# Moving the re-centring of quantized activations from GpSimd to ScalarE, and reordering one load queue

## The reference

```
B = xn @ W2 + b2;  C = xn @ W3 + b3                  # 16 columns each
delta = softplus(xn @ W1 + b1)                       # 1024 columns
s   = xn * delta * sum_n(B*C)                        # state-space layer, no recurrence left
xh  = xn @ Hadamard(1024) / 32
xq  = clip(round(xh / a), -8, 7) * a                 # a = max|xh| / 7, per token: 4 bits
wq  = ternary(weight) * scale                        # per output row
g   = silu(xq @ wq.T)
out = x + s * g
```

## Time and profile before

| engine | busy us | share of the span |
|---|---|---|
| TensorE (matmul) | 365.7 | 66% |
| VectorE | 384.0 | 69% |
| ScalarE | 307.3 | 55% |
| GpSimd | 327.3 | 59% |

### The profile page before, as it was taken

The page is one execution under the profiler, slowest core; times in us unless marked ns, Lnnn a source line. Parts: engine busy times, 40 slices in busy tenths (PEclk is TensorE's granted clock), DMA queues, the critical chain, the costliest instruction groups (busy, mean ns, idle before and its releaser), DMA issues.

```text
span 554.0 us, 7160 instructions; the slowest of 8 cores (548.4 to 554.0 us)
## 1 busy us (share of the span) xinstructions
PE 365.7 (66%) x1664; PEld 156.1 (28%) x1696; DVE 384.0 (69%) x632; ACT 307.3 (55%) x361; POOL 327.3 (59%) x215
## 2 busy tenths in 40 slices
PE   0005161996987888888888888888888885956400
PEld 0002131442333333333333333333333332422100
DVE  0508888466788887888788788887888866468450
ACT  0622232648676667666666676666666575444320
POOL 5000052151777777777776777776777778687664
PEclk9999565897989888888888888888888898888655
DMA  8993320252444444344444444444444232112101
GB/s 155 240 175 120 114 59 13 65 110 66 120 124 116 118 127 116 114 115 115 114 114 115 115 114 115 118 118 114 119 117 118 61 95 77 58 58 95 57 38 76
DMA packets 80971, 57.98 MB, mean 105 GB/s; under 512 B 70434, under 2 KB 70434, under 8 KB 80930
## 3 DMA queue, kind: packets, MB, share of 16 engines
q1 hardware_dynamic: 72914, 34.39, 27.7%
q0 software_dynamic: 8016, 23.14, 12.6%
HBM read 26.12 MB, written 16.78 MB: 77 GB/s over the span
## 4 chain that ended last, share of the span: by engine, by line
DVE 29%; POOL 26%; PE 18%; DMA 12%; issue 9%; ACT 2%; DVEq 1%; SPq 1%; POOLq 1%; ACTq 0%
POOL ob L33 8%; DVE t1b L33 8%; POOL t4b L33 8%; PE psO L292 7%; DMA xqT<-xqb 6%; PE psO L293 6%; POOL xqb L33 5%; DVE t3b L33 5%; DVE o3s L33 4%; DMA xb<-x 3%; DMA xnT<-xnb 3%; POOL vT L33 3%; DVE tbf L33 3%; POOL uT L33 3%; DVE prod L33 2%
## 5 line engine op out<-in xcount | busy, mean ns | idle before, releaser
L292 PE MATMUL psO<-ternT,xqT 128*128 128x512 bf16 x255 | 121.1, 475 | 68.9 <-DMA xqT<-xqb 66.9
L33 POOL TENSOR_TENSOR t4b<-t3b,o3s 128x1024 f32<-128x1024 f32 x32 | 75.1, 2347 | 85.5 <-DVE t3b L33 85.2
L293 PE MATMUL psO<-ternT,xqT 128*128 128x512 bf16 x256 | 121.4, 474 | 0.8 <-DMA xqT<-xqb 0.8
L271 PE MATMUL psZ<-W1c,xnT 128*128 128x512 bf16 x256 | 100.5, 393 | 0.5 <-DVE bcw L33 0.5
L272 PE MATMUL psZ<-W1c,xnT 128*128 128x512 bf16 x256 | 100.0, 391 | 0.0
L33 ACT ACTIVATE esb<-psO,nsa 128x1024 f32<-128x1024 f32 x32 | 35.7, 1115 | 113.9 <-DVE o3s L33 113.8
L33 POOL TENSOR_TENSOR xqb<-xqm,m160bf 128x1024 bf16<-128x1024 bf16 x32 | 70.4, 2201 | 45.5 <-ACT xqm L33 41.5
L33 DVE TENSOR_TENSOR t1b<-del,s 128x1024 f32<-128x1024 bf16 x32 | 79.0, 2470 | 4.5 <-ACT s L33 1.3
L33 POOL TENSOR_TENSOR ob<-xb,t4b 128x1024 f32<-128x1024 f32 x32 | 76.1, 2377 | 4.9 <-POOL t4b L33 0.4
L292 PEld LDWEIGHTS psO<-ternT,xqT 128*128 128x128 bf16 x256 | 30.0, 117 | 126.0 <-issue 111.0
L317 PE MATMUL psXH<-Hs,vT 128*128 128x512 bf16 x128 | 52.2, 408 | 14.3 <-ACT xqm L33 6.6
(11 more groups left out here) (53 smaller groups left out, 520.4 us busy)
## 6 DMA issues: line engine op xcount, KB each, us to landing
xb<-x SPq DMA_DIRECT2D x32, 512.0 KB, 3.8
out<-ob POOLq DMA_DIRECT2D x32, 512.0 KB, 3.0
wfst<-wf POOLq DMA_DIRECT2D x8, 512.0 KB, 3.6
W1c<-w POOLq DMA_DIRECT2D x8, 256.0 KB, 18.2
Hs<-hpk SPq DMA_DIRECT2D x1, 512.0 KB
xnT<-xnb SPq DMA_TRANSPOSE x32, 3.0
xqT<-xqb SPq DMA_TRANSPOSE x32, 3.1
m160bf<-m160p SPq DMA_DIRECT2D x1, 256.0 KB, 3.6
```

The costliest lines, as they stand in the source:

```text
L33: inst = fn(*a, **kw)
L271: pe.matmul(psZ1[:, 0:512], lh, W1c[ic][:, 0:512], start=(ic == 0), stop=False)
L292: pe.matmul(ps[:, 0:512], lh, ternT[:, ic * DM:ic * DM + 512], start=(ic == 0), stop=(ic == KC - 1))
L293: last = pe.matmul(ps[:, 512:1024], lh, ternT[:, ic * DM + 512:(ic + 1) * DM], start=(ic == 0), stop=(ic == KC - 1))
```

## The change

The subtraction of 160 is done by ScalarE, directly behind `xqm`, as an Identity with a per-partition bias of -160, and no longer by GpSimd. ScalarE then waits for the transpose of the tile before ahead of `xqb`, and no longer for `xqb` ahead of `xqm`. The input `m160p` and its tile are gone. On SP's queue the load of tile c+5 comes behind the transpose of `xnb`, still ahead of the transpose of `xqb`. Two constants (`identf`, `onesf`) are loaded that nothing reads, the staging tile of the ternarization has two buffers in turn, and the semaphore counts at the start are adapted.

```diff
@@ sync queue
+            sp.dma_start(out=identf[:], in_=identf_hbm[:]).then_inc(sWS, 16)
+            sp.dma_start(out=onesf[:], in_=onesf_hbm[:]).then_inc(sWS, 16)
-            sp.dma_start(out=m160bf[:], in_=m160_hbm[:]).then_inc(sC160, 16)
...
             for c in range(-4, nt + 4):
-                t = c + 5
-                if 5 <= t < nt:
-                    if t >= 11:
-                        sp.wait_ge(sVOUT, t - 10)
-                    sp.dma_start(out=xbuf[t % 11][:], in_=x_hbm[t * 128:(t + 1) * 128, :]).then_inc(sLDa[t % 11], 16)
                 t = c + 2
...
                                  transpose=True).then_inc(sTXNa[t % 3], 16)
+                t = c + 5
+                if 5 <= t < nt:
+                    if t >= 11:
+                        sp.wait_ge(sVOUT, t - 10)
+                    sp.dma_start(out=xbuf[t % 11][:], in_=x_hbm[t * 128:(t + 1) * 128, :]).then_inc(sLDa[t % 11], 16)
                 t = c - 1
@@ gpsimd
-                uq = c - 1
-                if 0 <= uq < nt:
-                    if uq == 0:
-                        g.wait_ge(sC160, 48)
-                    g.wait_ge(sRND, uq + 1)
-                    if uq >= 1:
-                        g.wait_ge(sTXQa[(uq - 1) % 2], 16 * ((uq - 1) // 2 + 1))
-                    gs.tensor_tensor(xqbf[:], xqm[:], m160bf[:], ALU.add, _inc=(sXQB, uq + 1))
@@ scalar
                     ac.wait_ge(sMX, u + 1)
-                    if u >= 1:
-                        ac.wait_ge(sXQB, u)
                     ac.activation(xqm[:], psXH[:], AF.Identity, scale=inv[u % 2][:],
                                   bias=c160s[:], _inc=(sRND, u + 1))
+                    if u >= 1:
+                        ac.wait_ge(sTXQa[(u - 1) % 2], 16 * ((u - 1) // 2 + 1))
+                    ac.activation(xqbf[:], xqm[:], AF.Identity, bias=nc160s[:], _inc=(sXQB, u + 1))
@@ vector, ternarization
-                    dv.tensor_single_scalar(cstage[0][:], wfstage[oc % 3][:],
+                    dv.tensor_single_scalar(cstage[oc % 2][:], wfstage[oc % 3][:],
```

More of the change, by code:

```diff
@@ L78, in build_nc @@
     nc160_hbm = nc.dram_tensor("nc160", [128, 1], F32, kind="ExternalInput").ap()
-    m160_hbm = nc.dram_tensor("m160p", [128, DM], BF16, kind="ExternalInput").ap()
     out_hbm = nc.dram_tensor("out", [tpc, DM], F32, kind="ExternalOutput").ap()
@@ L92, in build_nc @@
         onesbf = S("onesbf_s", [1, 128], BF16)
+        onesf = S("onesf_s", [1, 128], F32)
         identbf = S("identbf_s", [128, 128], BF16)
+        identf = S("identf_s", [128, 128], F32)
         c160s = S("c160_s", [128, 1], F32)
         nc160s = S("nc160_s", [128, 1], F32)
-        m160bf = S("m160bf", [128, DM], BF16)
         wfstage = [S(f"wfst{i}", [128, DM], F32) for i in range(3)]
-        cstage = [S("cst0", [128, DM], BF16)]
+        cstage = [S(f"cst{i}", [128, DM], BF16) for i in range(2)]
         ternbf = [S(f"tbf{i}", [128, DM], BF16) for i in range(3)]
@@ L128, in build_nc @@
         inv = mk1("inv"); dot = mk1("dot"); cc = mk4("cc")
-        mx = S("mx", [128, 1], F32); mxc = S("mxc", [128, 1], F32)
+        mx = S("mx", [128, 1], F32); mxc = S("mxc", [128, 1], F32); mxh = S("mxh", [128, 1], F32)
         msq = S("msq", [128, 1], F32); lnv = S("lnv", [128, 1], F32)
@@ L263, in _ @@
                         pe.wait_ge(sWG, 16 * 11)
-                        pe.wait_ge(sWS, 16 * 3)
-                        pe.wait_ge(sC160, 48)
+                        pe.wait_ge(sWS, 16 * 5)
+                        pe.wait_ge(sC160, 32)
                     pe.wait_ge(sTXNa[t % 3], 16 * (t // 3 + 1))
@@ L328, in prep_evac @@
                     ac.copy(ternT3[:, :, oc * 128:(oc + 1) * 128], psO3bf3, _inc=(sTEV, oc + 1))
-            ac.wait_ge(sC160, 48)
+            ac.wait_ge(sC160, 32)
             for c in range(-4, nt + 4):
@@ L390, in prep_cp @@
                     dv.scalar_tensor_tensor(ternbf[oc % 3][:], wfstage[oc % 3][:], swh_all[:, oc:oc + 1],
-                                            cstage[0][:], ALU.is_gt, ALU.subtract)
+                                            cstage[oc % 2][:], ALU.is_gt, ALU.subtract)
                     dv.tensor_single_scalar(ternbf[oc % 3][:], ternbf[oc % 3][:], sw_all[:, oc:oc + 1],
@@ L474 @@
         _CACHE["nc160"] = np.full((128, 1), -160.0, dtype=np.float32)
-        _CACHE["m160p"] = np.full((128, 1024), -160.0, dtype=ml_dtypes.bfloat16)
     nc = _CACHE["nc"]
@@ L480 @@
                   onesbf=_CACHE["onesbf"], onesf=_CACHE["onesf"], c160=_CACHE["c160"],
-                  nc160=_CACHE["nc160"], m160p=_CACHE["m160p"])
+                  nc160=_CACHE["nc160"])
     in_maps = [dict(common, x=np.ascontiguousarray(x[i * TPC:(i + 1) * TPC])) for i in range(NCORES)]
```

## The result

The changed kernel takes 512.24 us in the median of 8 runs (511.56 to 514.06), the kernel before 555.38 us in 10 runs taken with it. The ratio is 0.9225, with a 95% interval of 0.9211 to 0.9239: 7.8% faster. The profiled execution took 514.06 us, with a span of 512.5 us on its slowest core, core 4 (the cores lie between 506.3 and 512.5). Mean granted clocks rose from 0.845 to 0.852 to between 0.873 and 0.888.

A forecast was written before the change was run, and what follows sets the result against it. No single engine but a two-tile chain of waits through VectorE, GpSimd, the transposing DMA and TensorE was taken as bound. 555.56 − 38.5 (loop) − 3.8 (tail) − 0.3 (start) = 513.0, less 0.3 for the median: 512.7 us; range 499 to 533.

The forecast's parts named there:

- 25 periods: Main loop: the period falls from 13.69 to 12.15 us per tile, 38.5 us less over 25 tiles.
- Loop (b): VectorE and GpSimd in turn, one tile: 11.95 us, if prod is caught behind uT.
- TensorE's dip: TensorE's clock fall at its gap, then ahead of XH: expected in most periods, not all; 12.15 us period taken.
- R2: Rival: late bcw lets prod be caught behind vT; 13.25 us in such periods, 527 to 540 us; chance 0.20.
- The tail: Last three tiles: one period of 12.15 and two of 9.3 us in place of 34.5, 3.8 us less.
- loop (d): Serial tail o3s, t1b, t3b, t4b, ob and back: 9.3 us, deciding only after the last uT.
- The start: Before the loop: first xqb on ScalarE 1.25 us more, first t1b not held 1.6 less; together −0.3 us.
- R4: Slower rival: xqb on ScalarE costs over 3.46 us; with two table reloads 3.8, total 564 us; chance 0.05.
- SP's queue: Load of x issued between the xnT and xqT transposes: cost taken as nothing, up to 3.7 us delay for xqT.
- R5: Rival: xqT waits 3.7 us behind the load of x; 13.2 us per tile, 538 us; chance 0.06.
- R3: Rival: denser matmuls lose 3/16 of TensorE's clock; 12.4 us per tile, 519 us; chance 0.03.
- R1: Rival: ScalarE is the only bound, 11.4 us per tile, 494 us; chance 0.14.

The follow-up runs named there:

- two other edits: Changed kernel with prod reading one operand from PSUM and ScalarE's del moved behind xqb: 500.56 us; with the load of x also back ahead of the xnT transpose, 491.41 us.
- the row of edits: Changed kernel with prod reading one operand from PSUM, del behind xqb, and the load of x back ahead of the xnT transpose: 491.41 us.
- the fastest version: Changed kernel with prod from PSUM, del behind xqb, the old load order, and msq as tensor by per-partition scalar: 488.82 us.

## Why the prediction was right, step by step

The forecast was 512.7 us, the median is 512.24. That is closer than its steps were. From profile to profile 42.6 us were forecast and 41.5 measured (555.56 to 514.06), and the median lies 1.8 us below the profiled execution, where 0.3 was taken. By the `t4b` rows of both slowest cores the span's 41.5 us are made up so:

- *25 periods:* 342.29 − 311.48 = 30.8 us less, forecast 38.5. This is the term that was mis-sized. Loop (b) came out at 11.95 us to the hundredth in the short periods, with `prod` caught by `uT`, as taken. I allowed TensorE's dip 0.2 us on top, and expected it in most periods; it comes in 78 of 182 tiles, but where it makes `bcw` late it lets `prod` fall into the next operation, and costs 1.3 us. Nearly a third of the periods are long. Most of them are R2, with its 13.25 us (13.23 measured), mixed with the forecast and not an alternative to it; the fifth and the 22nd are the hold of `nmrs`, which no rival had. My objection to R2, that it corrects itself, held in part: on no core do the long periods take over, but core 4 has three of them in a row.
- *The tail:* 34.52 − 29.46 = 5.1 us less, forecast 3.8. Two steps are the 9.3 us of loop (d) (9.36 and 9.33), the third is 10.8 and not 12.15; in that step neither row sum nor square of a new tile is left, which fits, but no run tests it.
- *The start:* 5.8 us less by the first `t4b` (138.21 to 132.37), forecast 0.3. I had put the dropped 256 KB at "within ±1 us"; it is worth 3.2 by the run that loads it again. In the mean of the cores the first `t4b` comes 4.15 us earlier, 3.05 of them by the first product; the other 1.1 have the first `t1b` in them, which went from 2.1 to 2.8 us to 1.23. The rest of the 5.8 is the spread of the cores.
- *ScalarE:* `xqb` taken at 1.15 us, measured 1.148. R4 is out, as the price would have had to be 3.46.
- *The wait for `xqT`* is gone and XH waits for `xqm`, as forecast. By the run with the extra GpSimd operation and the one with `xqb` first, the chain of waits named the smaller of the two gains: with the wait it ended on (`xqT`) taken away and the hold left the gain was 0.7%, and putting the hold back into the changed kernel took most of its gain away.
- *SP's queue* at nothing: right in both kernels. `xqT` is issued 3.42 us behind the load, as taken, but lands in 3.7 us and not 3.1: R5's mechanism is real but covered. It decided as soon as two other edits took the cover away.
- *R3:* the stretch at 295 us has a granted clock of 1.00 with TensorE busy throughout. Of the 2720 stretches of 1 us between 140 and 480 us on the eight cores of the profiled execution 2246 have 1.00, 288 have 0.50, and the rest lie between, with no third value that stands out, 0.81 neither. The Trainium skill has the 13/16 in "TensorE: Matmul & The Clock Gate" under "Seeing it yourself", and not in the section that the prediction names. The trace of this execution does not agree with it, as far as TensorE here counts as dense.
- *R1* would have been true with the hold of `prod`, the gap ahead of XH and the queue's order mended: the row of edits comes to 11.50 us there, and to 11.46 with `msq`, R1's 11.4.
- *The range* held. Its lower end, a period of 11.6 us, was called half-way to R1; half-way from 12.15 to 11.4 is 11.8, or 503 us.
- *The signs:* three came out just outside what I wrote. The mean period is 12.34 us (12.0 to 12.3 said), ScalarE's idle time before `esb` 1.05 (under 1), and `prod` is above 1 us in most periods but 0.94 in the mean.

The terms for start and tail were 6.8 us too small together, the term for the loop 7.7 us too large. The mechanism of the gain was right; that the total came within 0.5 us was luck, because these two errors nearly cancel.

## What to carry to other kernels

When VectorE and GpSimd work side by side, look for VectorE operations whose duration varies: in this kernel their shortest row was their price and the rest a hold, and it went with the second SBUF operand. A 16-element product lost up to 1 us per tile in this way; giving it one operand from PSUM, and another product a per-partition scalar, took them out of GpSimd's way. Where two loops are within a few tenths of each other, forecast a mixture of periods and not their mean, and try again those edits that gave nothing once the bound has moved.

## What the hardware showed that was not expected

- The hold goes both ways: GpSimd's `uT` takes 1.96 us in place of 1.16 when it meets a running `t1b`.
- It depends on the operands and not on the size: `prod` took 0.94 us in the mean with two operands in SBUF and 0.18 with one of them in PSUM, and no longer in the fastest version, where it starts while `uT` runs; `msq`, one element per partition, 0.79 as a product of two tensors and 0.21, in the middle of `ob`, as tensor by scalar.
- A store went from 3.1 to 5.9 us to landing when the load of x was issued next to it, without any effect on the time of the changed kernel.
- Behind a gap of 1.97 us TensorE's clock fell from 1.00 to 0.50 at 290 us, behind one of 1.98 us at 315 it did not, and behind one of 0.52 us at 302 neither. Each fall cost 1.70 us.
